# Scores of both batches ahead of the weighted values, and maxima between the splits, in a pipelined attention block

## What is computed

```python
mod = silu(c) @ W_mod + b_mod
sh_msa, sc_msa, g_msa, sh_mlp, sc_mlp, g_mlp = split(mod, 6)
x = x + g_msa * attention(modulate(layernorm(x), sh_msa, sc_msa), W_qkv, W_out, b_out)
x = x + g_mlp * ff(modulate(layernorm(x), sh_mlp, sc_mlp), W1, b1, W2, b2)

def attention(x):                 # HEADS = 16, DH = 64
    q, k, v = split(x @ W_qkv, 3)
    attn = softmax(einsum('bqhd,bkhd->bhqk', q, k) * DH ** -0.5)
    return einsum('bhqk,bkhd->bqhd', attn, v) @ W_out + b_out
```

## Time and profile before

| what | value |
|---|---|
| median of 3 runs | 617.3 us |
| profiled execution | 617.99 us, its span on the core 616.5 us |
| mean granted clock of TensorE, share of full speed | 0.992 |
| TensorE matmul busy | 597.1 us, 97% |
| TensorE weight load busy | 540.1 us, 88% |
| VectorE busy | 511.8 us, 83% |
| ScalarE busy | 469.2 us, 76% |
| GpSimd busy | 288.9 us, 47% |
| chain that ended last, TensorE's share | 90% |

### The profile page before, as it was taken

One profiled execution on the slowest core, in us unless ns is written; L12 is line 12 of the kernel. 1 busy time (PEld: TensorE's weight loads), 2 busy tenths in 40 slices (PEclk: granted clock), 3 DMA queues, 4 the chain that ended last, 5 costly groups with the idle time before them and its releaser, 6 DMA issues.

```text
span 616.5 us, 17286 instructions
## 1 busy us (share of the span) xinstructions
PE 597.1 (97%) x5570; PEld 540.1 (88%) x5570; DVE 511.8 (83%) x1129; ACT 469.2 (76%) x1708; POOL 288.9 (47%) x353
## 2 busy tenths in 40 slices
PE   8899999999999999999999999699999999999996
PEld 8789999999999999999999998599887888888886
DVE  6789988898988988988988977678857788888876
ACT  4798888888888889789789789478775656656663
POOL 3336435435535535435435435446542544554551
PEclk9899999999999999999999999999998999999999
DMA  7210210210210210210210111223431122112101
GB/s 237 79 39 2 56 47 13 56 43 11 55 41 14 55 40 15 55 37 17 55 36 19 46 40 28 60 69 112 125 105 53 46 59 70 47 55 68 47 24 34
DMA packets 54678, 32.55 MB, mean 53 GB/s; under 512 B 15200, under 2 KB 52464, under 8 KB 54640
## 3 DMA queue, kind: packets, MB, share of 16 engines
q1 hardware_dynamic: 53008, 27.85, 16.6%
q0 software_dynamic: 1632, 4.21, 2.1%
HBM read 25.74 MB, written 6.31 MB: 52 GB/s over the span
## 4 chain that ended last, share of the span: by engine, by line
PE 90%; DVE 4%; ACT 3%; issue 1%; POOL 1%; DMA 0%; ACTq 0%; DVEq 0%; POOLq 0%
PE banks L658 10%; PE banks L688 9%; PE banks L671 9%; PE banks L1935 7%; PE banks L630 5%; PE banks L626 5%; PE banks L627 5%; PE banks L1348 4%; PE banks L1907 4%; PE banks L1921 3%; PE banks L711 2%; PE banks L642 2%; PE banks L1882 2%; PE banks L1895 2%; PE banks L713 2%; PE banks L712 2%
## 5 line engine op out<-in xcount | busy, mean ns | idle before, releaser
L567 POOL TENSOR_TENSOR late_blocks<-late_blocks,p_rsum 128x512 f32<-128x512 f32 x96 | 99.1, 1054 | 169.4 <-DVE p_rsum L969 169.4
L844 ACT ACTIVATE late_blocks<-banks,neg_max 128x128 f32<-128x128 f32 x384 | 137.5, 404 | 25.0 <-DVE neg_max L963 25.0
L844 ACT ACTIVATION_READ_ACCUMULATOR late_blocks<-banks,neg_max 128x1 f32 x384 | 93.7, 244 | 0.0
L825 ACT ACTIVATE wide<-banks 128x512 f32<-128x512 f32 x126 | 77.0, 612 | 6.4 <-PE banks L630 5.4
L963 DVE TENSOR_REDUCE neg_max<-banks 128x8 f32<-128x1024 f32 x64 | 76.5, 1195 | 1.1 <-PE banks L658 1.1
L626 PE MATMUL banks<-xT_hi,w_qkv_hi 128*128 128x256 f32 x256 | 77.2, 302 | 0.0
L630 PE MATMUL banks<-xT_hi,w_qkv_lo 128*128 128x256 f32 x256 | 72.0, 281 | 0.1
L627 PE MATMUL banks<-xT_lo,w_qkv_hi 128*128 128x256 f32 x256 | 71.6, 280 | 0.0
L658 PE MATMUL banks<-wide 64*128 64x128 f32 x1024 | 67.4, 282 | 1.3 <-ACT wide L825 1.3
L658 PEld LDWEIGHTS banks<-wide 64*128 64x128 f32 x1024 | 61.0, 191 | 7.1 <-issue 4.7
L844 ACT ACTIVATE third_p<-banks,neg_max 128x128 f32<-128x128 f32 x128 | 47.1, 389 | 21.7 <-DVE neg_max L963 21.7
(11 more groups left out here) (168 smaller groups left out, 1701.0 us busy)
## 6 DMA issues: line engine op xcount, KB each, us to landing
early<-in_mask SPq DMA_DIRECT2D x16, 220.0 KB
early<-in_mask SPq DMA_DIRECT2D x80, 44.0 KB
x_in<-in_x SPq DMA_DIRECT2D x16, 128.0 KB, 2.1
x_res<-in_x SPq DMA_DIRECT2D x16, 128.0 KB, 2.2
x_scratch<-x SPq DMA_DIRECT2D x16, 128.0 KB, 1.9
f_x_in<-x_scratch SPq DMA_DIRECT2D x16, 128.0 KB, 2.4
f_x_res<-x_scratch POOLq DMA_DIRECT2D x16, 128.0 KB, 2.7
x_scratch<-f_x POOLq DMA_DIRECT2D x16, 128.0 KB, 2.2
```

The lines of the kernel that those rows point to most:

```text
L567: pool.tensor_tensor(p[:, heads, :], p[:, heads, :], p_rsum[:, b, heads].unsqueeze(2).broadcast_to([128, 4, T]), ALU.mult).then_inc(p_read ...
L825: act.activation(qk_dst(name) if name[0] == "q" else v_dst(name), work_ps[bank], ACT.Copy).then_inc(bank_free[bank], 1)
L844: act.activation(p[:, m, :], s_ps[b][:, e, j, :], ACT.Exp, bias=neg_max[:, b, 4 * e + j:4 * e + j + 1], accum_out=p_sum[:, b, m:m + 1]).th ...
```

## The change

Two lists are written in another order. On TensorE the scores of both batches go in front of the weighted values of both batches, at the first and at the middle turn. On VectorE, `invert_sums` and the first `row_max` go in front of the first pair of splits, and the second `row_max` goes between the two pairs; `residual` goes behind both low parts. The start-up, `last_body`, and the lists of ScalarE, GpSimd and the DMA queue stay as they are.

```diff
--- before.py
+++ after.py
@@ -724,11 +724,11 @@
         def body(s):
             prev, nxt = step_from(s, -1), step_from(s, 1)
 
+            scores(s, 1, 0)
+            scores(s, 1, 1)
             if more(s, -1):
                 probs_v(prev, 1, 0)
                 probs_v(prev, 1, 1)
-            scores(s, 1, 0)
-            scores(s, 1, 1)
             turn_p(s, 0, 0)
             project_qk(s, "qk0a")
             project_qk(s, "qk0b")
@@ -742,10 +742,10 @@
                 project_out(s, 1)
             project_qk(s, "qk0d")
 
+            scores(nxt, 0, 0)
+            scores(nxt, 0, 1)
             probs_v(s, 0, 0)
             probs_v(s, 0, 1)
-            scores(nxt, 0, 0)
-            scores(nxt, 0, 1)
             if more(s, -1):
                 turn_back(s)
             turn_p(s, 1, 0)
@@ -1028,16 +1028,16 @@
         def body(s):
             prev, nxt, second = step_from(s, -1), step_from(s, 1), step_from(s, 2)
 
+            invert_sums(s, 0, 1)
+            row_max(s, 1, 0)
             if more(s, -1):
                 save_oT_high(prev, 1, 0)
                 save_oT_low(prev, 1, 0)
+            row_max(s, 1, 1)
+            if more(s, -1):
                 save_oT_high(prev, 1, 1)
-            invert_sums(s, 0, 1)
-            row_max(s, 1, 0)
-            if more(s, -1):
                 save_oT_low(prev, 1, 1)
             save_turned(s, 0, 0)
-            row_max(s, 1, 1)
             save_turned(s, 0, 1)
             if more(s, 2):
                 ln_moments(second)
@@ -1052,16 +1052,16 @@
             if more(s, -1):
                 gate(s)
 
+            invert_sums(s, 1, 1)
+            row_max(nxt, 0, 0)
             save_oT_high(s, 0, 0)
             save_oT_low(s, 0, 0)
+            row_max(nxt, 0, 1)
             save_oT_high(s, 0, 1)
-            invert_sums(s, 1, 1)
-            row_max(nxt, 0, 0)
+            save_oT_low(s, 0, 1)
             if more(s, -1):
                 residual(s)
-            save_oT_low(s, 0, 1)
             save_turned(s, 1, 0)
-            row_max(nxt, 0, 1)
             save_turned(s, 1, 1)
             edges.parts["sum_cells"](dve, s.n)
             if at(s, 1):
```

## The result

The changed kernel takes 726.27 us (median of 4 runs, 723.89 to 726.63), the kernel before 617.2 us beside it. The ratio is 1.1762, with a 95% interval of 1.1745 to 1.1779. The forecast was 720 us in a range of 690 to 742, slower with a chance of 0.95: the time lies 6 us above the forecast and inside the range. The profiled execution of the changed kernel is the fastest of its four, 723.89 us with a span of 722.4 us; against the 616.5 us before that is 105.9 us.

The account below looks back on a forecast made before the run. TensorE's list was taken to bound the kernel. Four waits, 6.6 us in each of 14 bodies plus 0.9 in body 0, gave 93 us; with 10 for clock falls, 720 us, range 690 to 742.

Parts of the forecast that it names:

- Term a: First turn: TensorE's second batch of scores waits for ScalarE's exponentials of unit (s, 0, 1), 1.8 us a body.
- term b: First turn: second transposes wait 0.3 us for bank A, `qk0b` 1.2 for bank D, freed by VectorE's last low part.
- term c: Middle turn: TensorE's first scores wait for ScalarE's copy of `qk0d`, 0.9 us a body.
- term d: Middle turn: TensorE's `qk1a` waits for bank C, which VectorE's `residual` now frees late, 2.4 us a body.
- The clock: TensorE's clock falls behind term d's wait in half of the bodies, 1.4 us each, 10 us in all.
- Rival 1: TensorE's clock holds after all four waits: 710 us, the lower end of the main case, whose chance was 0.75.
- Rival 2: The clock falls after term a's wait too, in every body: 749 us; chance 0.07.
- The places: Bodies 1 to 14 have all four terms, body 0 only term c; `last_body` is unchanged.
- Rival 3: VectorE's list gives no wait, only terms a and c stay: 656 us; chance 0.13, whole or in part.
- Rivals 4 and 5: Faster (chance 0.03), and no effect because the hardware looks past a waiting instruction (chance 0.02).
- rival 4: Faster: ScalarE's maxima waits vanish, 575 us, or 595 by 1.59 us a body of weight-load slack; chance 0.03.

Follow-up runs that it names:

- e1: Against the kernel before, both lists changed at the first turn only (where a body begins), middle turn as before: 665.19 us.
- e2: Against the kernel before, both lists changed at the middle turn only (behind `qk0d`), first turn as before: 679.63 us.
- e8: The changed kernel with four transposes in front of `qk1a` done four times instead of once, in bodies 1 to 14, as needless work: 717.84 us.
- e3: Against the kernel before, only TensorE's list changed, VectorE's as before: 709.02 us.
- e6: The changed kernel with the second maximum of each turn put back behind the first `save_turned`: 685.13 us.
- e4: Against the kernel before, only VectorE's list changed, TensorE's as before: 733.04 us.
- e7: Against the kernel before, TensorE alternates values and scores per batch at each turn; VectorE takes the first maximum between the splits: 629.68 us.
- e10: The kernel before with `turn_back` (two transposes) put between the two batches' scores at the middle turn: 621.89 us.

## Why the prediction was right

- **What bounds the kernel.** TensorE's list was the path and had no idle time in it; everything that now makes it wait shows in full. Shown by the four waits and by e1 and e2, whose bodies add up to that of the whole change.
- **Term a** (1.8, measured 1.74), **term b** (0.3 + 1.2, measured 0.28 + 1.24), **term c** (0.9, measured 0.95), **term d** (2.4, measured 2.37): each within 0.06 us. The prices came from starts, not from the durations shown, and each chain was followed through VectorE's or ScalarE's list to the wait that ends last.
- **That ScalarE and VectorE are back in time for the next turn**: right. No wait of TensorE that was not forecast appears in the steady bodies.
- **The clock**: half of 14 bodies at 1.4 us, 10 us. In the profiled execution it was 4 of 13 steady bodies, at 31.71 - 30.22 = 1.5 us each, and one more in the last block: some 7.5 us. That an idle time like d can make the clock fall was right, as e8 shows, and so was the price of one fall. The number of falls was a choice between none and one per body, with one case to go by; that it came out near is luck. The other three runs have a mean clock of 0.979 or 0.98 instead of 0.984 and are 2.2 to 2.7 us longer. A fall in body 0, as e2 and e8 have it, would fit, but these runs have no trace. Rival 1 (the clock holds) and the rule of the Trainium skill that the prediction sets beside it ("TensorE: Matmul & The Clock Gate", section "Why this matters for your kernels"), which asks for a longer idle time, were wrong for this case: idle times of 2.13 us were followed by falls. Rival 2 (also behind a) was wrong: e1 and e3 keep a, and show no fall in their steady bodies.
- **The places** were the weak step. "Body 0 has only c" gave it 0.9 us; together with a start-up that is 0.3 us later it cost 3.9. Up to the first `residual` the changed kernel is 72.06 - 61.32 = 10.7 us behind, of which body 1 has its 6.8. In body 0 TensorE waits 3.47 us at the scores for the copy of `qk0d`, where the earlier trace rows had 1.25 (ScalarE has no gap in front of that copy, and the values had covered 1.9 us of it), and 1.0 us at `v1b` for VectorE's low part, a wait of body 0 that the forecast did not look for:

```profile
43.01 0.50 PE L642 MATMUL banks<-w_qkv_hi,xT_hi 128*128 128x512 f32 x1 [1.02 <-DVE oT_lo L992]
```

- **The account** of the 105.9 us of the profiled executions: 14 bodies at 6.83 are 95.6, body 0 and the start-up 3.9, five falls of the clock 7.5, and behind the attention phase 1.1 less. The last is the clock again: the profiled execution before has a fall there that the one after does not have. Against 93 + 10 the restarts are 3.2 more, body 0 3.0 more, the clock 2.5 less and the last part 1.1 less, 2.6 us in all, so that misses of either sign partly cancel. The median is 6 us above the forecast, not 3, because the forecast took it to be 0.7 below the profiled execution and it is 2.4 above.
- **Rival 3** (VectorE's list gives no wait) was wrong as a whole, but e3 shows something close to it that I had not said: without VectorE's edit b and d would have come all the same. My forecast named the maximum between the splits as a cause of b; it costs 2.3 us a body when it is there (e6), yet with the old list another maximum is in its place. e4 shows the other half: VectorE's list alone costs more (733 us) than TensorE's alone (709) and than both together (726).
- **Rivals 4 and 5** (faster, no effect) had nothing: no run with earlier scores was faster than the kernel before, not even e7, whose steady bodies have no waits. The 1.59 us a body that rival 4 read as slack were none: a body with 3.3 us of waits more is 3.3 to 3.4 us longer (e1, e2).

## What to carry to other kernels

Where one engine's list has no gap, a reorder has nothing to win on it and can add waits to it, or longer steps (e10). Before moving a step forward, look up what each wait in front of it needs, and how long the work that stood there covered it; do the same for the step that is put off, whose result frees a buffer for someone. And take the cost from starts, through the whole chain of lists, not from the idle times of an engine that is not the path.

A wait of about 2 us on TensorE cost 1.5 us more here in the bodies in which the clock fell behind it, so compare the granted clock of each stretch before and after, not only the waits.

## What the runs showed of the hardware

- Each further change between matmuls on 64 rows, on 64 columns and on the full array came with some 0.17 us that the profile shows as longer steps, not as idle time (e7: 0.70 us for four a body; e10: 0.34 us for two).
- Whether TensorE's clock falls to its lower level (1.2 GHz) behind an idle time is not decided by that time's length alone: 3.5 us in body 0 were followed by full speed in the changed kernel and by half speed in e2 and e8; 2.1 us were followed by a fall in 4 of 13 bodies of the changed kernel, 6 of 13 of e2, and in all 13 of e4, where another idle time lay shortly ahead.
- Needless work in an idle time made the changed kernel 8.4 us faster (e8), by the falls of the clock that it took away.
